# The down product of a fused layer as seven half-size products, its block weights streamed through the weight ring

## The chip, the cores and the metric

The kernel runs on one core of one Trainium2 chip. The metric is the device time of one execution in microseconds. The engines of the core are named as the profile names them: PE (matrix products), DVE (vector), ACT (scalar, activation functions and copies), POOL (GpSimd), SP (which here only issues DMAs).

## What is computed

Eight sequences of 1024 rows of 512 numbers. A layer norm is followed by a causal linear attention with three decays, and by a gated feed-forward block whose weights are table look-ups:

```
xn = layernorm(x)
s  = attention(xn)                                # 3 heads of 128, decays, softmax gates
h  = silu(xn @ Wgate.T) * (xn @ Wup.T)            # 512 -> 1376
g  = silu(h @ Wdown.T)                            # 1376 -> 512: the down product
out = x + s * g
```

The three feed-forward weights are `lut[idx]` with 16 table values. Every product is made of 16-bit halves: each operand is split into a high and a low part, and three matrix instructions (high·high, high·low, low·high) replace one.

## The kernel before

**Setup.** The look-ups are made once, by one-hot products in 33 units (L1381). Sums of weight blocks for the gate and up products are added up in PSUM (L1403 to L1415), copied out by ACT (L765) and written to the DRAM tensor `blocks`. The down weights stay in SBUF as `wd_hi` and `wd_lo`, 11 chunks of 128 hidden columns, the last one of 96.

**Groups.** The 8192 rows are worked off in 16 groups of 512 rows (GT = 4 tiles of 128), two to a pass of the loop. A group has three stages on PE:

1. Projections (L1471): queries, keys, values and gate logits, 96 matrix instructions.
2. Products (L1585): gate and up, already in Strassen's form. The hidden chunks go in pairs, as sets s = 0 to 5; a set has seven products p = 0 to 6 of half-size blocks, each of 12 matrix instructions of 256 columns. Set 5 has a single chunk of 96, and its products have 6 instructions. Weight blocks come from `blocks` through `ring`, 14 slots that SP refills (L546). Between the products stand the attention's scores and retrievals (L1476 to L1478, L1503).
3. Down (L1614): for each of the four row tiles, 11 chunks times 3 instructions of 512 columns, then three instructions that apply the attention's output weights (`sum3` with `wo_hi`, `wo_lo`), and once the last retrieval.

**Around the products.** DVE combines the seven PSUM results of a set: `u2` (L1262), `u4` (L1272), `c22` (L1278), `c12` (L1284), `c21` (L1290), then forms the two halves of h, `h1` (L1297) and `h2` (L1304), which have two operands in SBUF. ACT copies the first product (L765, `first_copied`), applies the silu (L883, L889) and rounds h to its high part (`high1`, `high2`); POOL subtracts to get the low part (`low1` L690, `low2` L697). DVE's `u4` of a set overwrites what `h2` of the set before reads, so it waits for it, and PE's p = 5 waits for `u4`. POOL also makes the low part of the attention's probabilities (`low_probs`, L702), fades the state (L707), and prepares the next group's rows (L713) and their block sums (L721 to L730).

**Order.** Each engine's order is written out by hand: loops over n = 7s + p on all engines, and tables that place the other steps at an n (`ROWS1 = {16: 0, 24: 1}` places `rows1`, five small DVE operations from L1178 to L1187). An engine takes its instructions strictly in order.

**After the down stage.** ACT applies the silu (L935), DVE multiplies by the attention (L1356) and adds x (L1359), SP stores.

## Time and profile before

| | |
|---|---|
| median of 3 runs | 1871.83 us (1870.04 to 1873.10) |
| the profiled execution | 1871.58 us, span 1869.7 us |
| PE busy | 1834.5 us, 98% of the span |
| DVE, ACT, POOL busy | 1221.1, 654.2, 643.8 us |
| mean granted clock of PE | 0.996 |
| DMA | 275.97 MB, 148 GB/s |

The profile is of one execution. A page gives busy times, a row of the timeline gives the start of an instruction (or of several merged ones), its length, and in brackets how long the engine had been idle and what released it. A matrix instruction's length contains the time until its result is out; the next one starts earlier, so the pace of a series is read from the starts.

### The profile page before, as it was taken

How to read it: one execution, taken by the hardware profiler on the slowest of the kernel's cores; microseconds unless marked ns; L12 is line 12 of the kernel's file. 1: busy time of each engine (PE TensorE's matmuls, PEld its weight loads, DVE VectorE, ACT ScalarE, POOL GpSimd, SP SyncE). 2: the span in 40 equal slices, each digit the busy share in tenths (PEclk: the TensorE clock that was granted, in tenths of full speed). 3: DMA queues.
4: the chain of work that ended last, by engine and by line, in shares of the span. 5: the costliest groups of instructions: out<-in, count | busy, mean ns of one | idle time of the engine just before them, and what ended most of it. 6: DMA issues, size and time to landing. Idle time of an engine off the chain costs nothing.

```text
span 1869.7 us, 39469 instructions
## 1 busy us (share of the span) xinstructions
PE 1834.5 (98%) x14222; PEld 1252.1 (67%) x14222; DVE 1221.1 (65%) x2565; ACT 654.2 (35%) x1177; POOL 643.8 (34%) x641
## 2 busy tenths in 40 slices
PE   5889999999999999999999999999999999999999
PEld 1337668585866858486775948677584857768485
DVE  7877658484765748485684848567484857748364
ACT  2673334232423324242332414243341424334231
POOL 9303416061341606143160614325061432506031
PEclk9899999999999999999999999999999999999999
DMA  9956547365554736465473736557364655647250
GB/s 224 339 193 159 155 111 198 81 171 135 153 146 125 194 81 175 122 160 143 129 189 87 178 108 162 140 142 178 96 188 99 159 132 155 164 103 201 61 142 26
DMA packets 348854, 275.97 MB, mean 148 GB/s; under 512 B 216096, under 2 KB 253344, under 8 KB 348592
## 3 DMA queue, kind: packets, MB, share of 16 engines
q1 hardware_dynamic: 337664, 266.57, 53.8%
q0 software_dynamic: 11008, 6.89, 2.5%
q8 instruction: 126, 2.06, 0.5%
q14 instruction: 56, 0.46, 0.1%
HBM read 204.16 MB, written 30.93 MB: 126 GB/s over the span
## 4 chain that ended last, share of the span: by engine, by line
PE 94%; ACT 2%; POOL 1%; DMA 1%; SPq 1%; DVE 1%; issue 0%; POOLq 0%; DVEq 0%; ACTq 0%
PE F L1585 43%; PE F L1614 24%; PE B L1471 15%; PE B L1503 2%; PE B L1476 2%; PE B L1477 2%; PE B L1478 2%; POOL codes L616 1%; PE F L1381 1%; PE F L1476 1%; ACT ring L765 1%; PE F L1477 1%; PE F L1478 1%; DMA codes<-in_idx 1%; DMA blocks<-ring 1%
## 5 line engine op out<-in xcount | busy, mean ns | idle before, releaser
L1585 PE MATMUL F<-xtc,ring 128*128 128x256 f16 (+1 forms) x4224 | 497.7, 273 | 0.0
L1585 PEld LDWEIGHTS F<-xtc,ring 128*128 128x128 f16 (+1 forms) x4224 | 416.2, 100 | 42.3
L1614 PE MATMUL F<-wd_hi,region 128*128 128x512 f16 (+1 forms) x1408 | 429.2, 379 | 0.0
L1585 PE MATMUL F<-xt,ring 128*128 128x256 f16 (+1 forms) x3168 | 377.5, 273 | 0.0
L1585 PEld LDWEIGHTS F<-xt,ring 128*128 128x128 f16 (+1 forms) x3168 | 309.9, 100 | 34.5
L1614 PE MATMUL F<-wd_lo,region 128*128 128x512 f16 (+1 forms) x704 | 266.7, 379 | 0.0
L1614 PEld LDWEIGHTS F<-wd_hi,region 128*128 128x128 f16 (+1 forms) x1408 | 137.5, 98 | 162.7
L684 POOL TENSOR_TENSOR rstd<-var,nhalf 128x4 f32<-128x4 f32 x15 | 15.3, 1018 | 647.6 <-DVE var L966 647.6
L1356 DVE SCALAR_TENSOR_TENSOR region<-F,row_out,region 128x512 f32<-128x512 f32 x64 | 48.1, 751 | 291.2 <-ACT region L935 291.2
L690 POOL TENSOR_TENSOR region<-region 128x512 f16<-128x512 f32 x96 | 122.1, 1272 | 222.4 <-ACT region L765 222.4
L935 ACT ACTIVATE region<-F,scale_hf 128x512 f32<-128x512 f32 x64 | 44.0, 687 | 435.5 <-PE F L1614 435.5
L765 ACT ACTIVATE region<-region 128x512 f16<-128x512 f32 x192 | 113.8, 593 | 132.7 <-DVE region L1304 106.0
L1471 PE MATMUL B<-xt,a_hi 128*128 128x512 f16 x512 | 153.6, 382 | 1.1 <-issue 0.9
L702 POOL TENSOR_TENSOR region<-faded,region 128x384 f16<-128x384 f32 x64 | 68.1, 1064 | 226.6 <-ACT region L765 226.6
L1233 DVE SCALAR_TENSOR_TENSOR region<-B,region 128x512 f16<-128x512 f32 x64 | 44.3, 692 | 129.5 <-ACT region L765 129.5
L1471 PE MATMUL B<-a_hi,xt 128*128 128x387 f16 x512 | 128.7, 328 | 0.0
L883 ACT ACTIVATE region<-F,scale_down 128x512 f32<-128x512 f32 x96 | 62.2, 648 | 189.4 <-POOL region L697 126.8
L1614 PEld LDWEIGHTS F<-wd_lo,region 128*128 128x128 f16 (+1 forms) x704 | 68.9, 98 | 79.5
L697 POOL TENSOR_TENSOR region<-region 128x512 f16<-128x512 f32 x96 | 103.1, 1074 | 24.5 <-ACT region L765 24.5
L765 ACT ACTIVATE region<-B 128x512 f16<-128x512 f32 (+1 forms) x128 | 68.7, 537 | 110.5 <-PE B L1471 110.5
L1262 DVE TENSOR_TENSOR region<-region,F 128x512 f32<-128x512 f32 x96 | 61.4, 640 | 68.3 <-PE F L1585 68.2
L1476 PE MATMUL B<-region 128*128 128x128 f16 x552 | 99.0, 219 | 0.2 <-DVE region L1250 0.2
(206 smaller groups left out, 2956.0 us busy)
## 6 DMA issues: line engine op xcount, KB each, us to landing
ring<-blocks SPq DMA_DIRECT2D x546, 256.0 KB, 3.1
x_sb<-in_x SPq DMA_DIRECT2D x64, 256.0 KB, 3.6
out_y<-x_sb SPq DMA_DIRECT2D x64, 256.0 KB, 2.0
ring<-blocks SPq DMA_DIRECT2D x112, 128.0 KB, 2.5
blocks<-ring SPq DMA_DIRECT2D x35, 256.0 KB, 5.5
x_sb<-codes SPq DMA_DIRECT2D x10, 512.0 KB, 6.5
chalf<-codes SPq DMA_DIRECT2D x9, 512.0 KB, 6.5
xt<-codes SPq DMA_DIRECT2D x9, 512.0 KB, 8.4
```

The lines of the kernel that those rows point to most:

```text
L690: G_.tensor_tensor(h_lo[0:M, ms, 0:HALF], XC[s % 2][0:M, 0:w], h_hi[0:M, ms, 0:HALF], ALU.subtract).then_inc(s_hl1, 1)
L697: G_.tensor_tensor(h_lo[0:M, ms, HALF:GRP], SC[0:M, 0:w], h_hi[0:M, ms, HALF:GRP], ALU.subtract).then_inc(s_hl2, 1)
L702: G_.tensor_tensor(pr_half[:, 1], probs[:, :], pr_half[:, 0], ALU.subtract).then_inc(s_prl, 1)
L765: return nc.scalar.activation(dst, src, ACT.Copy, **kw)
L883: nc.scalar.activation(SC[0:M, 0:w], pair(0, s), ACT.Silu, scale=f_down[0:M, LUT:LUT + 1]).then_inc(s_sg1, 1)
L1262: V_.tensor_tensor(xc, xc, pair(1, s), ALU.subtract).then_inc(s_u2, 1)
L1471: ins = T_.matmul(bank[0:M, 0:cols], a, b, start=(n == 0), stop=(n == 3 * len(pairs) - 1))
L1476: T_.matmul(out, ah, bh, start=True, stop=False)
L1477: T_.matmul(out, ah, bl, start=False, stop=False)
L1478: return T_.matmul(out, al, bh, start=False, stop=True)
L1585: ins = T_.matmul(out_, a, b, start=fresh, stop=False, skip_group_check=True)
L1614: ins = T_.matmul(bf[:, :], a, b, start=(k == 0 and n == 0), stop=(k == FC - 1 and n == 2))
```

## The change

The down product of the first ten chunks is computed in Strassen's form: rows in two halves of 256, output columns in two halves of 256, and the two chunks of a set as the two halves of the inner dimension. The seven products (E11, E21, ET1, EN2, E22, ET3, EN4) are each summed over the five sets in PSUM. One product is 5 sets x 2 row tiles x 3 = 30 instructions of 256 columns. The eleventh chunk is computed directly, in four parts (`chunk`) of 6 instructions of 256 columns. The block weights are made in the setup, written to a new DRAM tensor `dblocks`, and come through the ring: 21 slots more per group. POOL makes four sums of quarters of h for each set (`h_sums1`, `h_sums2`) and their low parts at once (`h_sums_low`, 1024 columns), ACT their high parts (`h_sums_high`, 1024 columns).

```diff
+    ND = FC // 2
+    E11, E21, ET1, EN2, E22, ET3, EN4, E12 = range(8)
+    NE = 7
+    NSLOT = -(-ND // 2)
+    RING = 2 * NP
...
+    SUMD = {ET1: (E12, -1, E11), ET3: (E22, -1, E12), EN2: (ET1, -1, E22), EN4: (EN2, 1, E21)}
...
-        ROWS1 = {16: 0, 24: 1}
-        ROWS2 = {17: 0, 25: 1}
+        ROWS1 = {16: 0, 36: 1}
+        ROWS2 = {17: 0, 38: 1}
...
             def write_block(s, op):
+                if s == "down":
+                    for last in (ET3, EN4):
+                        sp.wait_ge(s_sum, NTH[("down", op), last, 1] + 1)
+                    sp.dma_start(dblocks[:, op // 2, :, op % 2].rearrange("e p c -> p e c"),
+                                 stage[op][:, 0:NE].rearrange("p e a c -> p e (a c)")).then_inc(s_dwr[op], 16)
+                    return
...
+            for k in range(ND):
+                sp.wait_ge(s_dwr[k], 16)
```

POOL (before, its part of a set was `low1(s - 1)` at p = 1, `low2(s - 1)` at p = 2, and `low_probs` in three sets; `low_probs` is now on DVE, and the next group's tiles 2 and 3 are prepared in the down stage):

```diff
+                    if p == 0 and s >= 2:
+                        h_sums_low(s - 2)
                     if p == 1 and s:
+                        h_sums1(s - 1)
                         low1(s - 1)
                     if p == 2 and s:
                         low2(s - 1)
+                        h_sums2(s - 1)
...
-                low1(NSET - 1)
-                low2(NSET - 1)
-                low_probs(GT - 1)
+                h_sums_low(ND - 1)
+                low1(ND)
+                low2(ND)
+                fade(GT - 1)
```

ACT:

```diff
                     act.wait_ge(s_hl1, q - 1 + 2 * FREE)
+                    if s >= 2:
+                        act.wait_ge(s_hs, (gi * ND + s - 1) * NHS)
                     copy(XC[s % 2][0:M, 0:w], pair(0, s)).then_inc(s_e1, 1)
...
                     if p == 5:
                         silu2(s)
+                        if s:
+                            h_sums_high(s - 1)
```

PE's down stage:

```diff
+                def down(e, bank, fresh=True, more=False):
...
+                    for k in range(NSLOT):
+                        n = NPG + e * NSLOT + k
+                        slot = ring_slot(g, n)
+                        pe.wait_ge(s_ring[slot // NP][slot % NP], ring_in(i, g, n))
+                        for s in range(2 * k, min(2 * k + 2, ND)):
+                            pe.wait_ge(low, c + s + 1)
...
+                            for j in range(2):
...
+                                for a, b in ((hh, wh), (hh, wl), (hl, wh)):
+                                    ins = T_.matmul(bank[:, j * HV:(j + 1) * HV], a, b, start=fresh, stop=False,
+                                                    skip_group_check=True)
...
+                down(E11, FB[1])
+                pe.wait_ge(s_sg1, gi * NSET + NSET)
+                down(E21, FB[0])
+                chunk(FB[0], 0, 0, False).then_inc(s_pf, 1)
+                retrieve(i, g, GT - 1)
+                pe.wait_ge(s_c21, gi * NSET + NSET)
+                down(ET1, FB[2])
+                attn_out(0)
+                pe.wait_ge(s_dc, gi * 4 + 1)
+                down(EN2, FB[1], False)
+                attn_out(1)
+                pe.wait_ge(s_c12, gi * NSET + NSET)
+                down(E22, FB[3])
+                chunk(FB[3], 0, 1, False).then_inc(s_pf, 1)
+                attn_out(2)
+                pe.wait_ge(s_dc, gi * 4 + 3)
+                down(ET3, FB[1], False)
+                attn_out(3)
+                pe.wait_ge(s_dc, gi * 4 + 2)
+                chunk(FB[2], 1, 1, False).then_inc(s_pf, 1)
+                pe.wait_ge(s_dc, gi * 4 + 4)
+                down(EN4, FB[1], False)
+                chunk(FB[1], 1, 0, False).then_inc(s_pf, 1)
```

DVE then adds partial results (`add_c11`, `add_partials`, `add_c12`, `add_c22`) and multiplies by the attention (`product_out`), POOL adds x (`finish`).

**What stands where on the engines.** POOL, from the low parts of set 3 to those of set 5, before (`region` is the buffer that holds h and its parts, L690 is `low1`, L697 `low2`):

```order
L697 TENSOR_TENSOR region<-region 128x2x256 [waits h2_hi_ready]
L689 REGISTER_ALU
L690 TENSOR_TENSOR region<-region 128x2x256 [waits h1_hi_ready]
L697 TENSOR_TENSOR region<-region 128x2x256 [waits h2_hi_ready]
L689 REGISTER_ALU
L690 TENSOR_TENSOR region<-region 96x256 [waits h1_hi_ready]
L697 TENSOR_TENSOR region<-region 96x256 [waits h2_hi_ready]
```

The same stretch after (L823 is `h_sums_low`, L809 to L819 are the four sums, L794 `low1`, L803 `low2`):

```order
L823 TENSOR_TENSOR region<-hs,region 128x1024 [waits h_sums_hi_ready]
L807 REGISTER_ALU
L808 REGISTER_ALU [waits h1_ready]
L809 TENSOR_TENSOR hs<-region 128x256 [waits h_sums_lo_ready]
L794 TENSOR_TENSOR region<-region 128x256 [waits h1_hi_ready]
L803 TENSOR_TENSOR region<-region 128x512 [waits h2_hi_ready]
L815 TENSOR_TENSOR hs<-region 128x256 [waits h2_ready]
L816 ISA
L817 TENSOR_TENSOR hs<-region,hs 128x256 [waits h_sums_ready]
L818 REGISTER_ALU
L819 TENSOR_TENSOR hs<-region,hs 128x256 [waits h_sums_ready]
L823 TENSOR_TENSOR region<-hs,region 128x1024 [waits h_sums_hi_ready]
```

Two operations a set have become seven. ACT around the start of set 5, before (the copy of 96x256 is the first copy of set 5):

```order
L883 ACTIVATE region<-F,scale_down 128x512 [waits h2_lo_ready]
L889 ACTIVATE region<-region,scale_down 128x512 [waits c12_ready]
L926 ISA
L765 ACTIVATE chalf<-tt 128x1024 [waits x_sums_ready]
L875 REGISTER_ALU
L765 ACTIVATE region<-F 96x256 [waits h1_lo_ready,product_in_psum]
L765 ACTIVATE region<-region 128x2x256 [waits h1_ready]
```

and after (L909 is every copy; the one from `hs` is `h_sums_high` of set 3):

```order
L1040 ACTIVATE region<-F,scale_down 128x512 [waits h2_lo_ready,product_in_psum]
L1046 ACTIVATE region<-region,scale_down 128x512 [waits c12_ready]
L1066 ISA
L909 ACTIVATE region<-hs 128x1024 [waits h_sums_ready]
L1026 REGISTER_ALU
L1027 REGISTER_ALU [waits product_in_psum]
L909 ACTIVATE region<-F 96x256 [waits h_sums_ready,h1_lo_ready]
L909 ACTIVATE region<-region 128x256 [waits h1_ready]
L909 ACTIVATE region<-region 128x512 [waits h2_ready]
```

The first copy of set 5 now stands behind a copy that waits for POOL's sums. DVE, from `h1` of set 4 to `u4` of set 5, before:

```order
L1297 SCALAR_TENSOR_TENSOR region<-region,scale_hf 128x512 [waits silu1_ready,c21_ready]
L1261 REGISTER_ALU [waits first_copied]
L1262 TENSOR_TENSOR region<-region,F 96x256 [waits product_in_psum]
L1304 SCALAR_TENSOR_TENSOR region<-region,scale_hf 128x512 [waits silu2_ready,h1_ready]
L1271 REGISTER_ALU [waits h2_ready,u2_ready]
L1272 TENSOR_TENSOR region<-F,region 96x256 [waits product_in_psum]
```

and after (L1518 is `h2`, L1486 `u4`, L1386 to L1395 are `rows1`):

```order
L1518 SCALAR_TENSOR_TENSOR region<-region,scale_hf 128x512 [waits silu2_ready,h1_ready]
L1385 REGISTER_ALU
L1386 TENSOR_REDUCE row_max<-mixed 128x1 [waits gated_ready]
L1387 REGISTER_ALU
L1388 TENSOR_SCALAR row_e<-row_max 128x1 [waits row_scale_step]
L1390 REGISTER_ALU
L1391 TENSOR_SCALAR row_e<-row_e 128x1 [waits row_scale_step]
L1392 REGISTER_ALU
L1393 TENSOR_SCALAR row_up<-row_e 128x1 [waits row_scale_step]
L1395 TENSOR_SCALAR row_down<-row_e 128x1
L1485 REGISTER_ALU [waits h2_ready,u2_ready]
L1486 TENSOR_TENSOR region<-F,region 96x256 [waits product_in_psum]
```

`rows1` has come between `h2` of set 4 and `u4` of set 5.

## Rows read from the trace of the kernel before

**Rows 1.** The page: busy time, 40 slices of PE in tenths, chain by engine.

```profile
PE 1834.5 (98%) x14222; PEld 1252.1 (67%) x14222; DVE 1221.1 (65%) x2565; ACT 654.2 (35%) x1177; POOL 643.8 (34%) x641
...
PE   5889999999999999999999999999999999999999
...
PE 94%; ACT 2%; POOL 1%; DMA 1%; SPq 1%; DVE 1%; issue 0%; POOLq 0%; DVEq 0%; ACTq 0%
```

**Rows 2.** Timeline of PE: start, length (us), engine, line, operation, out<-in, count.

```profile
261.71 1.48 PE L1585 MATMUL F<-xt,ring 128*128 128x256 f16 x12
...
263.02 1.15 PE L1585 MATMUL F<-xtc,ring 128*128 128x256 f16 x9
...
319.27 0.38 PE L1614 MATMUL F<-wd_hi,region 128*128 128x512 f16 x1
...
319.70 0.59 PE L1614 MATMUL F<-wd_hi,region 128*128 128x512 f16 x2
```

**Rows 3.** Chain that ended last, pieces: the projections of a group and of the next but one.

```profile
243.60 18.27 PE B L1471 x96
...
459.75 18.27 PE B L1471 x96
```

**Rows 4.** Windows: products, down; length, PE, PEld, DVE, ACT, POOL busy, clock, DMA share, GB/s.

```profile
261.70:319.30 57.60, 57.60 (x561) 51.49 (x559) 47.12 (x96) 25.76 (x44) 31.69 (x29) 1.00 0.66 175
319.30:351.50 32.20, 32.20 (x157) 14.81 (x154) 14.14 (x33) 4.73 (x9) 4.33 (x5) 1.00 0.43 103
```

**Rows 5.** Groups of POOL instructions by line and form: busy us, mean ns.

```profile
L690 POOL TENSOR_TENSOR region<-region 96x256 f16<-96x256 f32 x16 | 10.7, 668 | 26.0 <-ACT region L765 26.0
...
L697 POOL TENSOR_TENSOR region<-region 128x512 f16<-128x512 f32 x80 | 92.4, 1155 | 24.5 <-ACT region L765 24.5
...
L721 POOL TENSOR_TENSOR tt<-xp 128x256 f32<-128x256 f32 x30 | 21.7, 724 | 0.0
```

**Rows 6.** Timeline: a POOL and a DVE operation that meet, twice.

```profile
284.12 1.15 POOL L713 TENSOR_TENSOR xhat_half<-xp,xhat_half 128x512 f16<-128x512 f32 x1 [2.24 <-ACT xhat_half L765]
...
284.32 1.50 DVE L1297 SCALAR_TENSOR_TENSOR region<-region,scale_hf 128x512 f32<-128x512 f32 x1
...
322.40 2.93 DVE L1199 TENSOR_SCALAR mixed_half<-mixed,row_up 128x128 f16<-128x128 f32 x1
...
323.13 2.12 POOL L730 TENSOR_TENSOR chalf<-tt,chalf 128x1024 f16<-128x1024 f32 x1
```

**Rows 7.** Timeline: PE, DVE and ACT around the last set of products.

```profile
314.66 0.82 PE L1585 MATMUL F<-xt,ring 128*96 128x256 f16 x6
...
314.59 1.04 ACT L765 ACTIVATE chalf<-tt 128x1024 f16<-128x1024 f32 x1
...
316.51 0.74 DVE L1304 SCALAR_TENSOR_TENSOR region<-region,scale_hf 128x512 f32<-128x512 f32 x1
...
317.44 0.42 DVE L1272 TENSOR_TENSOR region<-F,region 96x256 f32<-96x256 f32 x1 [0.19 <-PE F L1585]
...
317.28 1.49 PE L1585 MATMUL F<-xt,ring 128*96 128x256 f16 x12
...
321.38 0.27 DVE L1178 TENSOR_REDUCE row_max<-mixed 128x1 f32<-128x128 f32 x1
```

**Rows 8.** Setup: its last window, two ACT copies, PE at its end.

```profile
116.00:134.00 18.00, 14.80 (x165) 5.61 (x158) 11.19 (x19) 14.43 (x29) 0.00 (x0) 0.99 0.32 118
...
129.97 0.38 ACT L765 ACTIVATE wd_hi<-F 128x256 f16<-128x256 f32 x1 [0.74 <-PE F L1381]
...
130.25 0.38 ACT L765 ACTIVATE wd_lo<-F 128x256 f16<-128x256 f32 x1
...
133.89 1.03 PE L1471 MATMUL B<-xt,a_hi 128*128 128x512 f16 x2 [0.23 <-issue]
```

**Rows 9.** Windows: the stretch of the setup with a low granted clock.

```profile
62.00:72.00 10.00, 7.67 (x55) 3.27 (x51) 6.89 (x12) 5.07 (x10) 1.16 (x2) 0.50 1.07 341
```

**Rows 10.** First group: DVE takes up the next x tiles.

```profile
147.30 1.87 DVE L974 BATCH_NORM_STATS2 stats<-x_sb 128x6 f32<-128x512 f32 x3
```

More of the change, by code:

```diff
@@ L80, in attention_ffn_kernel @@
             BASE[s] = len(UNITS) - 1
-            UNITS += [("last", 1), ("last", 0)]
+            UNITS += [("last", 1), ("last", 0), ("ends",)]
         else:
@@ L125, in attention_ffn_kernel @@
     PIECES.setdefault(22, []).append(("squares", 0, 0))
+    for k, (bank, chain, other) in CHAIN.items():
+        for n, u in enumerate(chain):
+            piece = (("down", k), (ET1, EN2, EN4)[n // 2], n % 2)
+            if u == int(u):
+                PIECES.setdefault(int(u), []).append(piece)
+            else:
+                MIDDLE.setdefault(int(u + 0.5), []).append(piece)
+        for part, u in enumerate(other):
+            PIECES.setdefault(u, []).append((("down", k), ET3, part))
     for p in PIECES.values():
         p.sort(key=lambda piece: -piece[2])
-    LATE = 2
-    ORDERED = [piece for u in range(NU + LATE) for piece in PIECES.get(u, ())]
+    LATE = 3
+    ORDERED = [piece for u in range(NU + LATE) for piece in MIDDLE.get(u, []) + PIECES.get(u, [])]
     NTH = {piece: n for n, piece in enumerate(ORDERED)}
@@ L148, in attention_ffn_kernel @@
                 HELD[NSET - 1, op] = n
-        else:
-            n += 4 if u[0] == "ends" else 2
-            if u[0] == "quad":
-                HELD[u[1], u[2]] = n
+        elif u[0] == "quad":
+            n += 2
+            HELD[u[1], u[2]] = n
+        else:
+            n += 4
+            for half in halves_of(u):
+                if half:
+                    HELD[("down", half[0]), half[1]] = n
         STORED.append(n)
@@ L158, in attention_ffn_kernel @@
             WRITES.setdefault(BASE[s] + u + SLOTS + LAG, []).append((s, op))
+    for k, (_, chain, other) in CHAIN.items():
+        WRITES.setdefault(int(max(chain[-1], other[-1]) + 0.5) + SLOTS + 2, []).append(("down", k))
     with ExitStack() as ctx:
@@ L645, in _ @@
             cast_set(SETS[0])
+            for u, c, col, w in COLUMNS["ends"]:
+                cast(u, c, col, w, s_cast_ends)
             for n in range(1, NSET):
@@ L834, in store_sum @@
                 elif s is None:
+                    act.wait_ge(s_dwr[0], 16)
                     copy(held(s, op, part), bank[:, :].rearrange("p (k t) -> p k t", k=2)).then_inc(s_sum, 1)
+                elif s not in SETS:
+                    copy(held(s, op, part), bank[:, 0:HV]).then_inc(s_sum, 1)
                 else:
@@ L841, in _ @@
             for b in range(NU + LATE):
+                for piece in MIDDLE.get(b, ()):
+                    store_sum(*piece)
                 if b < NU:
@@ new lines, in group @@
+                if not last:
+                    next_xhat(2)
+                add_c11()
+                if not last:
+                    next_xhat(3)
+                update_state(i, g, GT - 1)
+                mix(gi, g, GT - 1)
+                rows1(gi, GT - 1)
+                rows2(gi, GT - 1)
+                add_partials()
+                product_out(0)
+                add_c12()
+                product_out(1)
+                add_c22()
+                product_out(2)
+                product_out(3)
@@ L1377, in look_up @@
                 for j in range(CG):
+                    if j == 2:
+                        for piece in MIDDLE.get(b, ()):
+                            make(*piece)
                     pe.wait_ge(s_oh, b * CG + j + 1)
@@ L1453, in _ @@
                     look_up(b)
[L1454 to L1464 removed]
+                for piece in PIECES.get(b, ()):
+                    make(*piece)
             def three(bank, pairs, cols, M=P):
@@ L1578, in product @@
                             at0 = k * w + n * P
-                            sh, sl = (ring[:, s % 2, p, hl, at0:at0 + M] for hl in range(2))
+                            sh, sl = (ring[:, slot // NP, slot % NP, hl, at0:at0 + M] for hl in range(2))
                             if p in (0, 4, 5):
```

450 lines of the change are left out of this document (302 added, 148 removed).

## The prediction

> **What bounds the kernel now.** I read the page first: PE is busy for 98% of the span, and 94% of the chain that ended last is PE [rows 1]. DVE has 65%, POOL 34%. The windows by stage say the same more sharply: in the 57.6 us of products and in the 32.2 us of the down stage of a group, PE has no gap at all [rows 4]. One group takes half of the 216.15 us between two like pieces of the chain, 108.1 us [rows 3], and 16 of them are 1729 of the 1869.7 us; the other 140 us are the setup and the last store. So PE instructions saved in a group come off the time one for one, as long as nobody makes PE wait. The second thing to see is how near the others are: in the product stage DVE is busy for 47.1 of 57.6 us and POOL for 31.7 [rows 4].
>
> **The saving.** A 256-column instruction takes PE 109.2 ns from start to start (12 in the 1.31 us from 261.71 to 263.02), a 512-column one 215.5 (two in 0.43 us, from 319.27 to 319.70) [rows 2]. Before, a group's down stage has 4 x 11 x 3 = 132 of 512 columns, 28.45 us. After, it has 7 x 30 + 4 x 6 = 234 of 256 columns, 25.55 us. That is 2.9 us a group, **46.4 us** in 16 groups. The attention's four output sums and the last retrieval stay.
>
> **The setup.** Five chunk pairs get four sums each: 18 instructions of 256 columns, 90 in all, 9.8 us of PE at 109.2 ns. ACT gets 40 more copies of 256 columns and about 20 split ones, at 0.28 us from start to start [rows 8] some 12 us. Three of the five pairs fall into the first half of the setup, where PE waits for others anyway (5 tenths busy in the first slice of the page [rows 1]). The fourth falls into a full stretch, some 2 us, and the fifth is a chain of PE and ACT steps behind the last look-up that is one unit longer than the old one, some 3 us; PE and ACT are busy for 14.8 and 14.4 of the last 18 us [rows 8]. I take **6 us**, between 2 (nearly all hidden) and 12 (ACT's whole addition). The first group's x loads now stand in SP's queue behind the wait for the last `dblocks` write, and DVE wants them 13.4 us after the projections begin (133.89 to 147.30) [rows 8, 10]; 0 to 4 us, I take 1.
>
> **The ring.** 21 more slots a group, used at the pace of the products (12 instructions, 1.31 us a slot), with 14 slots in hand, some 18 us. DMA engines are at 0.43 of their time in the down stage and 0.66 in the product stage, which keeps up at that pace [rows 4]. I charge nothing. If SP came late with it, the same 18 us would have to be used up first.
>
> **POOL.** This is where the change pays. Before, POOL does two low parts a set: 2 x 1.16 = 2.3 us [rows 5]. After, it does four sums of 0.72, one low part of 256 columns (0.67, that of the 96x256 form), one of 512 (1.16) [rows 5], and one of 1024 (2.12) [rows 6]: 6.8 us. Five sets of that add 22.5 us to the product stage; three low probabilities (384 columns, so between the 0.67 and the 1.16, some 0.9 us each) go to DVE and half of the next group's preparation (two low parts of 512 columns and four sums, 5.2 us) goes to the down stage. So POOL's 31.7 us [rows 4] become about 46, plus what it waits for DVE. And POOL is now in a loop with ACT: sums of a set, ACT's copy of 1024 columns (1.04 [rows 7]), low part of 1024, next sums. That loop is 6.8 + 1.0 + 0.2 for the hand-overs, near 8 us, against 9.2 us that PE takes for a set. It fits, but late work is no longer caught up.
>
> **POOL and DVE.** The rows show that they exclude each other. DVE's L1297 (0.75 us when alone) began at 284.32 while POOL worked from 284.12 to 285.27, and it ended at 285.82, 0.55 us behind POOL [rows 6]. A small L1199 (0.28 alone) took 2.93 us and ended at 325.33, just after POOL's 1024-column operation that ended at 325.25 [rows 6]. Both have only SBUF operands. So each `h1` and `h2` can be held up by 2.1 us. The Trainium skill ("SBUF — State Buffer", section "SBUF: two separate sides") has the rule: a port pair is locked for a whole instruction by either a GpSimd operation or a DVE operation in a two-port mode or with two SBUF inputs. By that rule the new products and sums in the down stage and the low probabilities, all with two SBUF inputs, would be held up too; the rows of before show no such TENSOR_TENSOR beside a POOL operation.
>
> **Where PE then waits.** The tight place is p = 5 of set 5. Before, set 5 begins at 314.66, its p = 5 at 317.28 + 6 x 0.109 = 317.94, and the `u4` it waits for ends at 317.86 [rows 7]: no slack at all. Now count from the start of set 5, t = 0. POOL's sums of set 3 end about 0.4 (the loop above), ACT's copy about 1.45, and POOL's 1024-column low part runs from 1.5 to 3.6. DVE's `h2` of set 4 is ready to start at 2.1 and has to wait for it: it ends at 3.6 + 0.55 = 4.15. Then come the five operations of `rows1`, now placed between: 0.9 us (they begin at 321.38, the next operation at 322.40, and the last hand-over falls away, since `u4` doesn't wait for them [rows 6, 7]). `u4` takes 0.42 more and ends near 5.4. PE wants it at 3.3: **2.1 us**. Two more waits come the same way. In sets 3 and 4 the first copies on ACT stand behind the wait for POOL's sums, and `h2` behind POOL: together **1.1 us**. And the chunk of set 5 in the down stage needs `low2` of set 5, which stands behind the last 1024-column operation: the last sums end at 9.2, ACT's copy at 10.2, then 2.1 + 0.7 + 0.7 and hand-overs, 14.1; PE is there 60 instructions after set 5, at 6.7 + 6.55 = 13.3: **0.8 us**. Sum: 4.0 us a group, 64 us in 16 groups.
>
> I laid out a whole group of the changed kernel in this way, each engine's instructions in their order with the durations of the rows, to find these three places; the kernel before, laid out the same way, comes to 107.8 us a group against 108.1 measured, without a wait of PE. The layout is sensitive. With POOL's operations 5% shorter the three waits come to 2 us a group, with 5% longer ones to 6.
>
> **The sum.** 1871.6 (the profiled execution, 0.2 below the median, so it stands for it) - 46.4 + 6 + 1 + 64 = **1896 us**.
>
> **The rivals.**
>
> *POOL is no hindrance.* DVE's `h2` meets a gap of POOL, as most of the 192 `h1` and `h2` do now, and only `rows1` in the way of `u4` costs, some 0.9 us a group. Then 1871.6 - 46.4 + 7 + 14 = 1846 us. For it: POOL is idle for 26 of 57.6 us now, and the whole margin is the phase of one 2.1 us operation. Against it: the loop of 8 us in 9.2 us leaves POOL in work at nearly any moment.
>
> *It runs over.* The loop with its waits for DVE becomes longer than PE's set, lateness adds up from set to set, and PE waits for 6 us or more a group: 1871.6 - 46.4 + 7 + 96 = 1928 us, or more if PE's clock is cut. The clock was at half of full speed for 10 us of the setup, after waits of PE [rows 9]. A wait of 2 us in the middle of products may do that or not; each microsecond at 1.2 GHz costs half a microsecond.
>
> *Half of it.* POOL's operations are short enough that 2 us a group are lost: 1871.6 - 46.4 + 7 + 32 = 1864 us.
>
> **How the numbers follow.** The forecast (1880 to 1915) 0.50; POOL no hindrance (1838 to 1858) 0.20; half of it (1858 to 1880) 0.17; runs over 0.13. A difference under 0.2%, 3.7 us, can't be told from none. Faster by more than that: the first rival and half of the "half" case and a little, 0.30. Within: 0.06. Slower: 0.64. The range has to reach into both neighbours: from 1842 to 1928 it leaves some 0.1 out below and some 0.1 above.
>
> **What would show it.** Right: no PE gap in the projections and, but for the 0.8 us, none in the down stage; in set 5 a gap of PE before an L1846 released by DVE L1486; `h2` (L1518) with a mean well over the 0.74 us of rows 7; POOL near 48 us of the product stage. Wrong: a PE gap released by a ring DMA, a down stage with gaps behind `down_partial_copied` or the transposes of the attention, L1885 slower than 109 ns a piece, or a setup that ends later than 142 us.

## Result and profile after

The changed kernel takes 1937.8 us (median of 4 runs, 1929.0 to 1942.2) against 1870.9 us; the ratio is 1.0353, 95% interval 1.0334 to 1.0373. It is slower, as forecast, but by 67 us and not by 25, and outside the range.

The profiled execution took 1939.05 us, its span is 1937.2 us. Taking the start of the first instruction of each stage in PE's timeline, group by group, and adding up over the 16 groups gives (the waits at the start of a projection stand in the down stage before it):

| us | before | after | change | forecast |
|---|---|---|---|---|
| setup, to the first projection | 133.9 | 139.7 | +5.8 | +7 |
| projections | 294.0 | 306.2 | +12.1 | 0 |
| products | 915.8 | 976.8 | +61.0 | +51 |
| down | 521.4 | 504.4 | -17.0 | -34 |
| from the start of the last PE instruction to the end | 4.5 | 10.1 | +5.6 | 0 |
| sum | 1869.7 | 1937.2 | +67.5 | +25 |

The page of after: PE's share has fallen from 98% to 94%, and more transfers carry instructions (q8 and q14).

```profile
PE 1826.7 (94%) x15944; PEld 1421.2 (73%) x15944; DVE 1287.3 (66%) x2629; ACT 803.3 (41%) x1445; POOL 1025.4 (53%) x1041
...
q8 instruction: 142, 2.33, 0.5%
q14 instruction: 92, 0.75, 0.1%
...
L823 POOL TENSOR_TENSOR region<-hs,region 128x1024 f16<-128x1024 f32 x80 | 175.4, 2193 | 63.2 <-ACT region L909 63.2
...
L1518 DVE SCALAR_TENSOR_TENSOR region<-region,scale_hf 128x512 f32<-128x512 f32 x96 | 120.2, 1252 | 0.6
```

The page of before had 126 and 56 such transfers:

```profile
q8 instruction: 126, 2.06, 0.5%
q14 instruction: 56, 0.46, 0.1%
```

PE's waits in after (engine, line, what it waited for: us in total, times, longest; "issue" is time in which the engine waited for nothing that the profile shows). The third row is in the setup, where before has a similar one.

```profile
PE F L1846 <- DVE region L1486: 47.6, 46, 2.2
PE B L1731 <- issue: 17.5, 7, 3.0
PE F L1638 <- DVE region L1216: 16.0, 4, 13.2
PE B L1731 <- DVE region L1447: 4.7, 7, 0.7
...
PE F L1866 <- POOL region L803: 1.5, 9, 0.2
```

The first row is what the prediction was about. Set 5 of group 14, the place of the forecast's "tight place" (timelines of POOL, DVE and PE; start, length, idle time before):

```profile
1783.46 2.13 POOL L823 TENSOR_TENSOR region<-hs,region 128x1024 f16<-128x1024 f32 x1 [1.17 <-ACT region L909]
```

```profile
1784.02 2.11 DVE L1518 SCALAR_TENSOR_TENSOR region<-region,scale_hf 128x512 f32<-128x512 f32 x1
1786.06 0.27 DVE L1386 TENSOR_REDUCE row_max<-mixed 128x1 f32<-128x128 f32 x1
...
1786.81 0.14 DVE L1395 TENSOR_SCALAR row_down<-row_e 128x1 int32<-128x1 int32 x1
1786.87 0.41 DVE L1486 TENSOR_TENSOR region<-F,region 96x256 f32<-96x256 f32 x1
```

```profile
1787.34 0.93 PE L1846 MATMUL F<-xt,ring 128*96 128x256 f16 x6 [2.15 <-DVE region L1486]
```

POOL's 1024-column low part runs until 1785.59, `h2` ends at 1786.13, `rows1` takes until 1786.95, then comes `u4`, and PE has waited 2.15 us. In a row of before like this, PE waited for nothing [rows 7].

The second row of the waits was in no one's forecast. It is PE at the end of every second group:

```profile
583.38 0.27 PE L1866 MATMUL F<-wd_lo,region 96*128 96x256 f16 x1
583.49 0.27 PE L1866 MATMUL F<-wd_hi,region 96*128 96x256 f16 x1
586.56 0.60 PE L1731 MATMUL B<-xt,a_hi 128*128 128x512 f16 x1 [2.79 <-issue]
```

The waits of 2.99, 2.79, 2.56, 2.96, 2.97 and 2.87 us stand before groups 2, 4, 6, 8, 10 and 12. Those are the six places where the loop over pairs of groups jumps back. Between the two groups of one pass there is none, and none before group 14, where the loop ends and its last pass, written out, follows. Before had 0.3 us or less there. While PE stands, the DMA engines are busy for over 90% of the time and carry two packets of instructions (DMA view of 583 to 587 us):

```profile
q1 hardware_dynamic: 651, 1.19, 90.2%
q8 instruction: 1, 0.02, 1.6%
q14 instruction: 1, 0.01, 0.9%
```

In the same place before, at the jump at 567.73 us, no data moved and two packets of instructions did (DMA view of 564 to 568 us):

```profile
q8 instruction: 2, 0.03, 3.4%
```

And the clock falls to 1.2 GHz behind most of these gaps, and behind some of the waits in set 5 (windows; the third number from the end is the granted clock, 0.50 is 1.2 of 2.4 GHz):

```profile
551.00:553.00 2.00, 1.83 (x14) 1.69 (x15) 1.84 (x6) 0.00 (x0) 2.00 (x4) 0.84 0.53 190
553.00:556.00 3.00, 3.00 (x17) 2.10 (x16) 2.91 (x7) 2.02 (x4) 1.75 (x3) 0.54 0.73 202
584.00:586.00 2.00, 0.00 (x0) 0.00 (x0) 0.69 (x1) 0.57 (x1) 0.62 (x1) 1.00 0.84 301
586.00:588.00 2.00, 1.44 (x4) 0.58 (x5) 0.00 (x0) 0.00 (x0) 0.64 (x1) 0.62 0.75 282
588.00:590.00 2.00, 2.00 (x7) 0.66 (x5) 0.00 (x0) 0.00 (x0) 0.00 (x0) 0.52 0.57 207
```

Between 552 and 1791 us there are twelve such stretches of 3.4 us, 1.7 us lost in each, 20 us: five behind a jump, seven behind the wait in set 5. The kernel before has none there.

### The profile page after: what moved, and what is told of

It is laid out like the page before. It is cut to its first block and busy times, and to the rows that moved or that the text cites. A ratio compares the mean times of both kernels' runs of the same rounds, so it can differ in the third digit from the quotient of the medians.

```text
span 1937.2 us, 45221 instructions
## 1 busy us (share of the span) xinstructions
PE 1826.7 (94%) x15944; PEld 1421.2 (73%) x15944; DVE 1287.3 (66%) x2629; ACT 803.3 (41%) x1445; POOL 1025.4 (53%) x1041
## 3 DMA queue, kind: packets, MB, share of 16 engines
HBM read 277.56 MB, written 35.52 MB: 162 GB/s over the span
## 5 line engine op out<-in xcount | busy, mean ns | idle before, releaser
L1846 PEld LDWEIGHTS F<-xtc,ring 128*128 128x128 f16 (+1 forms) x4224 | 416.5, 100 | 45.9 <-DVE region L1498 3.5
L1885 PE MATMUL F<-ring,region 128*128 128x256 f16 x3360 | 392.2, 277 | 0.0
L1885 PEld LDWEIGHTS F<-ring,region 128*128 128x128 f16 x3360 | 333.4, 99 | 52.9
L823 POOL TENSOR_TENSOR region<-hs,region 128x1024 f16<-128x1024 f32 x80 | 175.4, 2193 | 63.2 <-ACT region L909 63.2
L839 POOL TENSOR_TENSOR x_sb<-x_sb,region 128x512 f32<-128x512 f32 x64 | 81.0, 1265 | 192.0 <-DVE region L1585 192.0
L1731 PE MATMUL B<-xt,a_hi 128*128 128x512 f16 x512 | 158.4, 392 | 22.2 <-issue 17.5
L909 ACT ACTIVATE region<-region 128x256 f16<-128x256 f32 x192 | 94.4, 500 | 166.5 <-DVE region L1518 166.5
L909 ACT ACTIVATE region<-F 128x512 f32<-128x512 f32 (+2 forms) x176 | 95.4, 550 | 150.9 <-PE F L1885 112.4
L1447 DVE SCALAR_TENSOR_TENSOR region<-B,region 128x512 f16<-128x512 f32 x64 | 44.3, 692 | 162.2 <-ACT region L909 161.8
L1476 DVE TENSOR_TENSOR region<-region,F 128x512 f32<-128x512 f32 x96 | 61.5, 641 | 135.2 <-ACT region L909 94.0
L1731 PE MATMUL B<-a_hi,xt 128*128 128x387 f16 x512 | 128.7, 328 | 0.0
L803 POOL TENSOR_TENSOR region<-region 128x512 f16<-128x512 f32 x96 | 112.8, 1175 | 28.5 <-ACT region L909 28.5
L1518 DVE SCALAR_TENSOR_TENSOR region<-region,scale_hf 128x512 f32<-128x512 f32 x96 | 120.2, 1252 | 0.6
L909 ACT ACTIVATE region<-B 128x512 f16<-128x512 f32 (+2 forms) x144 | 75.3, 525 | 108.0 <-PE B L1731 105.3
L909 ACT ACTIVATE region<-hs 128x1024 f16<-128x1024 f32 x80 | 84.2, 1052 | 71.0 <-POOL hs L819 71.0
L1731 PEld LDWEIGHTS B<-xt,a_hi 128*128 128x128 f16 x512 | 50.2, 100 | 86.3 <-issue 25.9
```

The lines of the kernel that those rows point to most:

```text
L803: G_.tensor_tensor(out, f, hi, ALU.subtract).then_inc(s_hl2, 1)
L823: G_.tensor_tensor(h[:, 1, s, ET1:ET3 + 1], hs[:, :, :], h[:, 0, s, ET1:ET3 + 1], ALU.subtract).then_inc(s_hsl, 1)
L839: G_.tensor_tensor(to, to, block, ALU.add).then_inc(s_yr, 1)
L909: return nc.scalar.activation(dst, src, ACT.Copy, **kw)
L1447: V_.scalar_tensor_tensor(out=qk_lo[:, j], in0=B[j % 2][:, :], scalar=2.0 ** QP, in1=qk_hi[:, j], op0=ALU.mult, op1=ALU.subtract).then_inc ...
L1476: V_.tensor_tensor(xc, xc, pair(1, s), ALU.subtract).then_inc(s_u2, 1)
```

## The experiments

**1. What is the wait at the jump?** The same edit in both kernels writes the loop out, on all five engines:

```diff
-            with pe.Fori(0, NB - 1) as i:
+            for i in range(NB - 1):
```

> The changed kernel with its loop written out: 16 groups in a row, no branch between them, everything else as it was. In the changed kernel PE stood for 2.6 to 3.0 us before the first projection of groups 2, 4, 6, 8, 10 and 12 (17.1 us), which are the six places where the loop jumps back, and after five of them the clock was at half speed for 3.4 us (8.5 us lost). Theory 'the jump': PE has to fetch its program anew after the jump. Then all six waits and the five clock cuts go, with the 0.7 us waits for L1447 behind them: about 1908 us (1904 to 1914). Rival 'the data': the first projection waits for something that the other engines or a transfer deliver late at the end of every second group; then the waits stay and the time is 1938 us.

> Control: the kernel before with its loop written out in the same way. PE's waits at its six jumps are 0.3 us or less in the trace, so both theories say no change: 1870 us, within 2.

After: 1899.3 us, ratio 1.0167 (1.0135 to 1.0199) to before. No L1731 waits for anything; PE's waits are

```profile
PE F L1846 <- DVE region L1486: 46.0, 46, 2.2
PE F L1866 <- POOL region L803: 2.9, 14, 0.2
PE F L1846 <- DVE region L1498: 1.9, 7, 0.3
```

So 38.5 us of the 67 go with the loop. By the stages 40.5 us went from the groups of the profiled execution: 17.1 of waits at the jump, ten of the twelve clock cuts (17 us), and some 6 more, mostly the waits for L1447 behind the jump (4.7). That is more than expected, since five of the cuts in set 5 went as well, though its waits stayed at 2.15 us. Those five (8.5 us) are not shown to be the jump's doing: the number of cuts differs between executions of one kernel (the written-out one took 1896.2 us at a mean clock of 0.997 and 1908.9 at 0.989), and a kernel without the loop, in experiment 4, has seven. At the same mean clock of 0.993 the two kernels took 1929.0 and 1901.5 us, a difference of 27.5.

The edit also takes out the instructions with which each engine computes, in the loop, the values that it waits for (45221 records in the trace of after, 41684 written out). In the kernel before this and the covered jump come to little: the control, before written out, is 1866.7 us, ratio 0.9979 (0.9969 to 0.9990), 4 us faster, where no change was expected; the gain is spread over setup, products and down (1.7 to 1.9 us each in the profile). The packets of instructions fell too, on q8 from 142 to 129 in after and from 126 to 114 in before: the kernel before also fetched at its jumps.

**2. Why does the same jump cost nothing before?** Two differences at that place: the last instructions are half as long, and the DMA engines are busy. One at a time, in the kernel before:

```diff
-                        for n, (a, b) in enumerate(((hh, wh), (hh, wl), (hl, wh))):
-                            ins = T_.matmul(bf[:, :], a, b, start=(k == 0 and n == 0), stop=(k == FC - 1 and n == 2))
+                        for v0, v1 in (((0, HV), (HV, V)) if d == GT - 1 else ((0, V),)):
+                            for n, (a, b) in enumerate(((hh, wh), (hh, wl), (hl, wh))):
+                                ins = T_.matmul(bf[:, v0:v1], a, b[:, v0:v1], start=(k == 0 and n == 0),
...
```

```diff
                     sp.dma_start(out_v[row_group(i, g)][:, t], x_sb[:, g, t]).then_inc(s_y[t], 16)
+                    if d == 2 and g == GPB - 1 and not last:
+                        sp.wait_ge(s_refill, 16 * (6 * i + 1))
+                        for m in range(6):
+                            sp.dma_start(refill[m], blocks[0, m]).then_inc(s_refill, 16)
```

> The kernel before, with the last of the four row tiles of each down stage made in 66 instructions of 256 columns in place of 33 of 512: the same work and nearly the same time on PE (+0.1 us a group), but the last instructions ahead of the jump are half as long, as in the changed kernel. Theory 'short instructions': PE's sequencer runs a fixed number of instructions ahead, so it reaches the jump only half as long before the queue runs dry: six waits of 2 to 3 us, some with a clock cut, 1884 to 1898 us. Rival 'busy DMA engines': the fetch is slow only because transfers of weights and rows fill the DMA engines at that moment; here they are idle, no wait over 0.5 us, 1871 to 1873 us.

> The kernel before, with six additional copies of 256 KB from one DRAM tensor to another, issued by SP after the third row tile's store of every second group, so that they run while PE comes to the jump; instructions on PE as before. Theory 'busy DMA engines': six waits of 2 to 3 us, 1884 to 1898 us. Rival 'short instructions': PE reaches the jump early enough, waits under 1 us, 1870 to 1875 us. If both this run and the one with short instructions stay at 1871, it takes both together.

> The kernel before with both changes at its jump: the last row tile in 66 instructions of 256 columns, and the six copies of 256 KB that run while PE comes to the jump. Alone, short instructions gave six waits of 1.5 to 1.9 us (10.8 us), copies six of 1.0 to 2.0 us (9.7 us), each +12 us. Theory 'both count, and add up' (less time in PE's queue, and a slower fetch): waits of 3 to 4 us, as in the changed kernel (2.6 to 3.0) or a little more, most of them with a clock cut of 1.7 us: 1895 to 1908 us. Rival 'the slower of two': waits under 2.2 us, 1882 to 1886 us.

Short instructions: 1882.7 us, ratio 1.0061 (1.0044 to 1.0077). Copies: 1882.2 us, 1.0063 (1.0046 to 1.0080). Both: 1899.5 us, 1.0163 (1.0146 to 1.0180). PE's wait at the first projection in the three:

```profile
PE B L1471 <- issue: 11.2, 7, 1.9
```

```profile
PE B L1479 <- issue: 10.1, 7, 2.0
```

```profile
PE B L1479 <- issue: 20.3, 7, 3.6
```

(Six of the seven stand at a jump.) Each alone had been set against the other as rivals; both count and they add up: 1.8 and 1.6 us a jump, together 3.3, with a clock cut behind five of the six. The changed kernel has both, and 2.6 to 3.0. So the wait at the jump, and 30 us of time (1899.5 against 1869.5), are reproduced in a kernel that has nothing of Strassen in its down stage.

The packets show how. At each of the 30 jumps (six in before, in these three kernels and in after) a packet of 16 KB of instructions starts on q8, and the first projection follows 2.8 to 3.3 us behind its start (3.8 to 4.1 at three jumps with copies, where the packet itself took 2.0 us and not about 1). What differs is when it starts, against the end of PE's work (from the trace's DMA records and PE's timeline, six jumps each):

| us | packet starts | PE's wait |
|---|---|---|
| before | 2.9 to 3.0 ahead | 0 to 0.3 |
| short instructions | 0.9 to 1.4 ahead | 1.5 to 1.9 |
| copies | 1.0 to 2.3 ahead | 1.0 to 2.0 |
| both | 0.1 ahead to 0.7 behind | 3.1 to 3.6 |
| after | 0.3 ahead to 0.1 behind | 2.6 to 3.0 |

Before, the same fetch lay under PE's work. With instructions half as long the packet starts half as far ahead, or less; with copies it takes longer or starts later. The Trainium skill ("Runtime: NRT & Kernel Launch", section "Instruction fetch mechanics") says that a taken branch whose target is not in the fetched window makes the engine fetch the page by DMA before it goes on; the runs agree, with 0 to 3.6 us exposed on PE. That short instructions and copies delay the packet is worked out from these runs; what stands in PE's queue shows in no row.

**3. Is POOL's length what PE waits for in the products?** All further kernels have the loop written out, unless said.

```diff
-        ROWS1 = {16: 0, 36: 1}
-        ROWS2 = {17: 0, 38: 1}
+        ROWS1 = {16: 0, 24: 1}
+        ROWS2 = {17: 0, 25: 1}
```

> The changed kernel with its loop written out, and rows1 and rows2 of the second row tile put back from n = 36 and 38 to n = 24 and 25, where the kernel before has them. The five small DVE operations (0.9 us) then no longer stand between h2 of set 4 and u4 of set 5. Theory of the prediction: PE's wait of 2.15 us at p = 5 of set 5 falls to 1.2 to 1.7 us, and the wait for low2 before the chunk grows from 0.2 to about 0.8 us, since POOL's late work is less hidden: 3 to 6 us less than with the loop written out alone (1899), 1893 to 1896 us. Rival: DVE has room for rows1 in the time in which it waits anyway, and only POOL sets the end of u4: 1899 us.

1894.8 us, ratio 1.0127 (1.0110 to 1.0144). The wait in set 5 is 1.50 us in place of 2.15, the chunk's 1.04 in place of 0.20: both steps as expected. They cancel almost: in the second group the product stage went from 61.5 to 60.5 us and the down stage from 29.7 to 30.5. `rows1` is 0.65 us of the chain, and taking it out only hands the time on to the next wait. Of the 4.5 us, 3.4 may be two clock cuts that the trace no longer shows.

```diff
-                    G_.tensor_tensor(h[:, 1, s, ET1:ET3 + 1], hs[:, :, :], h[:, 0, s, ET1:ET3 + 1],
+                    G_.tensor_tensor(h[:, 1, s, ET1:ET1 + 1], hs[:, 0:1, :], h[:, 0, s, ET1:ET1 + 1],
                                      ALU.subtract).then_inc(s_hsl, 1)
```

> The changed kernel with its loop written out, with POOL's low part of the four sums made for one of the four alone: 256 columns (0.63 us) in place of 1024 (2.13 us). The low parts of the other three sums are left out of the computation. It takes 1.5 us a set from the loop POOL sums, ACT copy, POOL low part, and shortens what h2 on DVE can be held up by. Theory 'POOL': h2 (L1518, mean 1.25 us in the changed kernel) comes down to 0.8 to 0.9 us, PE's waits in sets 3 and 4 and before the chunk go, and at p = 5 of set 5 about 1 us stays, rows1: 1850 to 1858 us. Rival 'DVE and ACT': the waits come from the longer lists of DVE and ACT, POOL's length doesn't matter: over 1890 us.

This kernel leaves out the low parts of three of the four sums, so its output is not that of the others; it is there for the time alone. 1844.0 us, ratio 0.9860 (0.9843 to 0.9876), 6 us under the expected range. Taking 1.5 us a set from POOL takes 55 us from the kernel. `h2` is back to 0.89 us, and one wait a group is left, of 0.4 us where 1 was expected:

```profile
L1518 DVE SCALAR_TENSOR_TENSOR region<-region,scale_hf 128x512 f32<-128x512 f32 x96 | 85.0, 885 | 0.6
```

```profile
PE F L1846 <- DVE region L1486: 6.8, 16, 0.4
```

Its down stages sum to 473.8 us against 519.7 of before written out: -45.9, the saving that the prediction had put at 46.4.

**4. Lock or load?** Both `h2` being held and POOL being late come from the 1024-column operation. Cut in two, it holds `h2` for less, but costs POOL more:

```diff
-                    G_.tensor_tensor(h[:, 1, s, ET1:ET3 + 1], hs[:, :, :], h[:, 0, s, ET1:ET3 + 1],
-                                     ALU.subtract).then_inc(s_hsl, 1)
+                    G_.tensor_tensor(h[:, 1, s, ET1:ET1 + 2], hs[:, 0:2, :], h[:, 0, s, ET1:ET1 + 2],
+                                     ALU.subtract)
+                    G_.tensor_tensor(h[:, 1, s, ET1 + 2:ET3 + 1], hs[:, 2:4, :], h[:, 0, s, ET1 + 2:ET3 + 1],
+                                     ALU.subtract).then_inc(s_hsl, 1)
```

> The changed kernel with its loop written out, and POOL's low part of the four sums made in two operations of 512 columns in place of one of 1024. Question: who gets in when DVE's h2 is waiting and POOL has the next operation ready. Theory 'DVE gets in between': h2 (L1518, mean 1.25 us) can be held up by one half only, its mean falls below 1.1 us, PE's wait at p = 5 of set 5 falls from 2.15 to about 1.3 us, and although POOL needs some 0.15 us more a set the time falls from 1899 to 1884 to 1895 us. Rival 'POOL keeps it': h2 stays as long or gets longer, and the additional POOL time lengthens the loop: 1900 to 1925 us.

1925.3 us, ratio 1.0294 (1.0277 to 1.0312): 26 us slower than with one operation, the rival's number, though by the other theory's mechanism. DVE does get in between: `h2`'s mean is 0.88 us (first row), and POOL's second half then waits for DVE (1.48 us against 1.22).

```profile
L1520 DVE SCALAR_TENSOR_TENSOR region<-region,scale_hf 128x512 f32<-128x512 f32 x96 | 84.4, 879 | 0.6
```

```profile
L825 POOL TENSOR_TENSOR region<-hs,region 128x512 f16<-128x512 f32 x80 | 118.7, 1484 | 0.0
...
L823 POOL TENSOR_TENSOR region<-hs,region 128x512 f16<-128x512 f32 x80 | 97.8, 1223 | 51.2 <-ACT region L911 51.2
```

So one must look at the loop POOL sums, ACT copy, POOL low part: half a microsecond a set more in it (2.7 us in place of 2.2) weighs more than `h2` 0.4 us sooner. In the profiled execution PE's waits are 17 us longer, and there are seven clock cuts in the groups against two (8.5 us more); how much of the 26 us is the clock's stays open, since an execution at a mean clock of 0.996 also took 1923.2 us. The waits moved to the chunk and to the first copies:

```profile
PE F L1848 <- DVE region L1488: 37.1, 31, 1.8
PE F L1868 <- POOL region L803: 22.9, 13, 2.1
PE F L1848 <- ACT region L911: 8.1, 22, 0.4
```

**5. Moving the work instead of leaving it out.** First POOL's late work was moved: the low part of the next rows' sums into the down stage, `low1` to DVE at p = 2, the last retrieval ahead of the chunk, `rows1` early.

> The changed kernel with its loop written out, all of the computation, and four steps moved: the low part of the next rows' sums (x_sums_low of pair 0, 2.1 us of POOL) from set 3 into the down stage, rows1 and rows2 of the second tile to n = 24 and 25, the low part of h1 (low1, 256 columns) from POOL to DVE at p = 2 behind u4, and on PE the last retrieval ahead of the first chunk. If POOL's lateness is what PE waits for, as the prediction has it, 1.0 to 1.4 us of waits a group are left of 3.4: 1852 to 1862 us. If DVE becomes the late one with low1, the waits stay at 3 us a group or more: 1890 to 1900 us.

> The same four steps moved, with the loop as it is in the changed kernel. Theory: the jump costs the same as before (six waits of 2.6 to 3 us, clock cuts of 1.7 us behind most of them, 26 to 38 us against the loop written out), since it has nothing to do with POOL; the clock cuts at p = 5 of set 5 go with the waits there: 1884 to 1896 us. Rival: with a shorter list of late work the PE's sequencer comes to the jump earlier and the waits there shrink too: below 1880 us.

1906.5 us (1.0190, 1.0173 to 1.0207), and with the loop 1959.2 us (1.0469, 1.0451 to 1.0487): both slower than the kernels they came from. In the products the waits fell (2.15 to 0.8 us in set 5, in all 3.0 to 1.9 us a group, where 1.0 to 1.4 were expected), but the down stage had a new one:

```profile
PE F L1744 <- DMA region<-mixed_half: 26.4, 22, 2.9
PE F L1854 <- DVE region L1487: 23.9, 31, 1.1
```

SP's queue shows why (timeline of SP in the down stage): the transpose for PE's `attn_out` at 348.02 stands behind two others. One of them (`xtc`) needs the step that I had moved, and had moved with it behind seven loads of the ring.

```profile
332.11 8.30 SPq L628 DMA_DIRECT2D ring<-dblocks  x7
340.56 2.72 SPq L573 DMA_TRANSPOSE xtc<-chalf  x1
343.40 2.92 SPq L573 DMA_TRANSPOSE xt<-xhat_half  x2
346.38 1.52 SPq L624 DMA_DIRECT2D ring<-blocks  x3
348.02 1.19 SPq L573 DMA_TRANSPOSE region<-mixed_half  x1
```

Then POOL's order at the end of set 5 alone (with `rows1` early), and the rearrangement with the moved step kept in set 5:

```diff
-                h_sums_low(ND - 1)
                 low1(ND)
                 low2(ND)
+                h_sums_low(ND - 1)
                 fade(GT - 1)
```

> As the kernel with rows1 and rows2 early (loop written out, 1894.8 us), and on POOL low1 and low2 of set 5 (96 rows, 256 columns each) ahead of the low part of the sums of set 4 (1024 columns), which PE needs only two products later. The chunk then doesn't wait for the 1024 columns: its wait of 1.04 us in each group goes, 1876 to 1880 us. Rival: the 1024 columns come too late for the products with sums (L1885 waits for POOL L823), the wait only moves: 1890 us or more.

> As the rearranged kernel with its loop written out, but x_sums_low of pair 0 stays in the product stage, at n = 37 (set 5) in place of the down stage, so that SP turns it at once as in the changed kernel, and low1 and low2 of set 5 go ahead of the low part of the sums of set 4. In the rearranged kernel (1906.5 us) PE waited 26 us for the transposes of mixed_half (22 times, up to 2.9 us), which stood behind those of the sums in SP's queue. Theory: that new queue was the whole difference to what was expected; those waits go, and waits of 1.0 to 1.5 us a group for L1486 and the like stay: 1850 to 1862 us, faster than both kernels. Rival: SP is late for another reason (the ring's 21 more loads), the transposes are still waited for: 1880 us or more.

> The same steps moved, with the loop as in the changed kernel. The rearranged kernel cost 52.7 us more with the loop than without, the changed one 38.5. Theory: the jump (six waits of 2.6 to 3.3 us, the waits for L1447 behind them, clock cuts of 1.7 us) costs 35 to 45 us again: 1888 to 1905 us. Rival: without the late work at the end of a group PE's sequencer gets to the jump sooner, under 25 us: below 1882 us.

Chunk first: 1892.4 us (1.0114, 1.0097 to 1.0130), a gain of 2 us on `rows1` early alone, and not of 17. The chunk's wait of 15.6 us is gone, but the transposes of `mixed_half` are now waited for (9.4 us): PE comes to them earlier. Second rearrangement: 1894.6 us (1.0121, 1.0104 to 1.0138), with the loop 1949.8 us (1.0417, 1.0399 to 1.0436). The transposes were most of the difference (26.4 to 3.9 us), but the retrieval, placed first, now waits for the low probabilities on DVE, 13.6 us. Both misses have one form: a step was freed of one wait, and its next one, unseen so far, stood right behind. With the loop the two rearranged kernels lose 53 and 55 us, more than the 38.5, though the jump's own waits are 16.6 and 18.4 us. Part of the rest is more clock cuts; part is waits for DVE's `c22` (L1493, 10.7 us against 2.6), and these don't come from the jump: 0.41 us stand in each of the 14 groups of the loop, some 62 us behind its first projection. In group 5 DVE's `low1`, just ahead of it, took 1.38 us with the loop and 0.42 without. What makes the two meet there stays open.

At last the long operation went to DVE, behind `h1` (this is DVE's side, without the last call behind `h2`; POOL's calls are gone, and `rows1` is early):

```diff
+                    if p == 0 and s >= 2:
+                        h_sums_low(s - 2)
                     if p == 1:
                         u2(s)
```

> The changed kernel with its loop written out, all of the computation, the low part of the four sums (1024 columns) on DVE behind h1 in place of POOL, and rows1 and rows2 at n = 24 and 25. It takes 2.13 us a set from POOL and gives DVE an estimated 1.1 us (from L1518's 0.75 us for 512 columns alone, and L1491's like), while h2 no longer finds POOL in a 1024-column operation. Theory 'POOL's length': waits of PE in the product stage come down from 3.4 us to 0.5 to 1.2 us a group, 1858 to 1868 us, and the transposes of mixed_half may be late by some us in all as in the other faster versions. Rival 'DVE is the next bound': h1 and u4 are late instead, 2 us a group or more, over 1885 us.

> The same with one exchange in SP's queue in the down stage: the transpose of mixed_half for the third tile ahead of those of the next rows' tiles 2 and 3, which wait for POOL. Theory 'SP stands in order behind POOL': the waits of PE for mixed_half (9.4 us in the kernel with the chunk first) go, 2 to 10 us less than the run beside it. Rival 'the transposes are slow because the ring's transfers fill the DMA engines': the waits stay, the same time within 2 us.

1874.8 us (1.0028, 1.0018 to 1.0039) and 1873.0 us (1.0015, 1.0004 to 1.0027). On DVE the operation takes 1.32 us, more than the estimate of 1.1, against 2.2 on POOL. The waits for `u4` came down from 46.0 us (33.2 with `rows1` early alone) to 15.4, inside the expected band; the time is 7 us over it. What remained, in the run with SP's order unchanged:

```profile
PE F L1851 <- DVE region L1483: 15.4, 31, 1.1
PE B L1768 <- DVE mixed L1376: 8.4, 16, 0.5
PE F L1741 <- DMA region<-mixed_half: 5.3, 10, 0.9
```

The exchange in SP's queue took 3 us of its last row away (5.3 to 2.1), hardly more than the runs scatter: inconclusive as a time (1.7 us, under the 2 to 10 expected), right as a mechanism. The second row names one DVE step:

```diff
-        MIX = {11: 0, 18: 1}
+        MIX = {11: 0, 18: 1, 39: 2}
...
-                mix(gi, g, GT - 2)
```

> As the kernel with the sums' low part on DVE and the exchange in SP's queue (loop written out, 1873.0 us), and mix of the third tile (four DVE operations) back from the start of the down stage to n = 39, in set 5, where DVE waits for PE. In the run before, PE waited 0.53 us in each group for exactly this step ahead of the last retrieval (L1768 for L1376, 8.4 us in all), and each wait costs some 0.17 us more than its length. Theory: these go, 1860 to 1864 us, below the kernel before (1869.5) and its version with the loop written out (0.998 of it). Rival: the step makes h1 or u4 of set 5 late, the wait moves there: 1870 to 1876 us.

1858.0 us, ratio 0.9938 (0.9925 to 0.9952). This version computes everything and is faster than the kernel before by 12 us, and than before written out (1866.7, measured another time) by some 9. The row of L1768 is gone:

```profile
PE F L1850 <- DVE region L1483: 15.2, 31, 1.1
PE F L1740 <- DMA region<-mixed_half: 3.0, 7, 0.8
```

## Why the prediction was wrong in size

**The saving**: right. 256-column instructions kept 109 ns (30 of L1885 in 3.27 us), and with POOL's load taken off the down stages were 45.9 us shorter.

**The setup**: right, +5.8 against 6, and +6.4 between the two written-out kernels, though part of that is luck: in the other written-out versions it ends anywhere from 139.4 to 142.4 us. PE waited for none of the first group's x loads.

**The ring**: right as far as it went. PE never waits for a ring load, although 73 MB more are read from HBM (277.56 against 204.16 MB). The new transfers cost elsewhere: at the jump, and in what stands in SP's queue around the transposes.

**POOL**: 42.0 us of a product stage of 61.7, not 46; it was late all the same.

**Where PE waits**: the place, the chain and the sizes were right. Forecast 2.1, 1.1 and 0.8 us a group; measured 2.15 (2.09 with the loop), 0.8 to 1.3, and 0.2. Counted from the start of set 5 (group 4 written out), POOL's low part ran from 1.5 to 3.6, `h2` ended at 4.2 and `u4` at 5.3 us; the forecast had 1.5 to 3.6, 4.15 and 5.4. Two errors here cancel: the chunk waits 0.6 us less, and each wait costs PE 0.18 us more than its idle time (group 4 written out: product stage 60.25 against 56.81 us, waits of 2.89 us in three places). Without the jump one group takes 109.2 us, as forecast; the written-out kernel, 1899.3 us, lies 3 us from the forecast of 1896, partly by chance, since writing out alone gives 4 us and the end costs 5.6.

**The sum**: this is the step that failed. It took a group as a closed cycle, 16 times, and had no term for what lies between two passes of the loop; "no PE gap in the projections" was one of its signs of being right. Writing the loop out gives 38.5 us: in the profiled execution 17 of waits at the jump, 6 behind it, and 17 of clock cuts, of which half stand at a jump. The trace of before has waits of 0.2 to 0.3 us at three jumps; the fetch behind them was covered by 512-column instructions and idle DMA engines, and the change took both covers away. A second term was put at nothing, the clock: the prediction left open whether a wait of 2 us cuts it, and seven cuts stand behind its own "tight place", 12 us in the profiled execution. A third missing term is the end, +5.6 us: the last tile goes through ACT, DVE and then POOL (1.26 us, where DVE took 0.69), and from the last result two stores of 256 KB take 7.0 us to the end, where it was one and 2.5. This was read from the timeline and not tried.

**The rivals**: "it runs over" gave 1928 us or more and a cut clock, near the measured time. The cuts came, but its main reason did not: the waits in the products do not add up from set to set. Its price for a cut was right (1.7 us for 3.4 us at half clock). "POOL is no hindrance" gave 1846 us; the kernel with a quarter of the low part took 1844, but with its loop written out.

**POOL and DVE**: the exclusion holds, also for a TENSOR_TENSOR with two SBUF inputs such as the low probabilities (L1425, 0.89 us in the mean), which before could not show: 17 of the 64 met no POOL operation and took 0.55 us, the other 47 ended 0.41 us behind one. This agrees with the rule of the Trainium skill ("SBUF — State Buffer", section "SBUF: two separate sides") that the prediction cites. The split run adds that the one that waits gets in at the next boundary of an instruction.

## What to carry to other kernels

Where a change makes PE's instructions shorter or fills the DMA engines, look at what follows a jump of the loop: a wait "issue" that is 0.3 us now can be the end of a covered fetch (the DMA view shows its packet ahead of it), and writing the loop out, or having long instructions ahead of the jump, is a cheap test. When an engine other than the bound one gets more work, add up the loop that its results go round, not its share of busy time; and after each wait that is removed, look for the next one behind it before counting the gain.

## What was not expected of the hardware

- A taken jump costs PE 0.3 us or less before, 1.5 to 1.9 us with 256-column instructions ahead of it, 1.0 to 2.0 us with 1.5 MB of copies under way, 3.1 to 3.6 us with both. Where the loop ends, before group 14, PE did not wait.
- With the same wait of 2.15 us in set 5, the clock was cut seven times with the loop and twice without (profiled executions). In the split run, without the loop and with waits of 1.8 us for DVE and 2.1 for POOL, it was cut seven times. What else decides it stays open.
- POOL and DVE take turns at instruction boundaries: a POOL operation of 1024 columns in two pieces lets a waiting DVE operation in (`h2` 1.25 to 0.88 us) and pays 0.5 us for it.
